# Ternary weights turned in pairs, rows turned by transfers, a split store and earlier norms

## The chip, the cores and the metric

One NeuronCore of a Trainium2 chip runs the whole program. The metric is the device time of one execution in microseconds; lower is better. TensorE, VectorE (DVE), ScalarE (ACT), GpSimd (POOL) and SyncE (SP, which issues most transfers) run side by side and are ordered by semaphores only.

## The reference

Four residual blocks on x of 1250 rows by 1024 (fp32), each on layer-normalised rows:

```python
x = x + layernorm(x) @ W.T + bias            # W scattered from 41250 edge weights at [src, dst]
x = x + moe(layernorm(x))                    # 8 experts, top 2, capacity 314, 1024 -> 512 -> 1024, relu
h = layernorm(x) @ gW.T + gb                 # dense linear layer
x = x + segment_sum(norm * h[col], row)      # normalised adjacency with self loops, norm from degrees
x = x + bitlinear(gelu(bitlinear(layernorm(x), w1)), w2)   # 1024 -> 4096 -> 1024

def _quant_weight(w):
    s = jnp.clip(jnp.mean(jnp.abs(w)), EPS, None)
    wq = jnp.clip(jnp.round(w / s), -1.0, 1.0) * s
    return w + jax.lax.stop_gradient(wq - w)
def _bitlinear(x, w):
    return jnp.einsum('bsi,oi->bso', _quant_act(x), _quant_weight(w))
```

So each feed-forward weight becomes -1, 0 or +1 times one scale: it is +1 above s/2 and -1 below -s/2. Activations are rounded to 8-bit integers by row.

## The kernel before

Rows are cut into NT = 10 tiles of 128; x stays in SBUF. The 1024 features make KD = 8 blocks of 128, the hidden 4096 make KF = 32. Every engine has its instruction stream written out by hand; the order in each stream and the semaphores set the order of the work. Values that need more than 16 bits are carried as two fp16 parts, high and low.

Stages in time: edges are turned into dense matrices (one-hot matmuls, L816 and L819, whose moving operand `o_key` has a step of SLOTS = 2 fp16 elements); first linear layer; router; eight experts; mixture of the experts' results; second linear layer; aggregation over the adjacency, with the ternary weights made beside it; feed-forward.

**Linear layers** (`normalised`, four functions of that name or its inlined form). Per tile n with buffer u = n % 2: POOL computes `rstd`; DVE `norm` writes `xn` (L1625); ACT `high` writes `xh` (L1230); DVE `low` writes `xl` (L1630). TensorE `transposes` turns `xh` and `xl` by eight 128x128 transposes each into PSUM banks 4 and 5 (L889, L895); ACT `copy_high` and DVE `copy_low` bring them to `xth` and `xtl` (L1234, L1634). `product` (L907) then runs 48 matmuls of 512 columns. TensorE does the transposes of tile i + 1 ahead of the product of tile i. DVE takes the result out (L1665 in the first layer, `h32` at L1933 in the second), and in the first layer statistics follow. In the first layer TensorE and ACT run tiles 0 to 7 and DVE tiles 0 to 5 as hardware loops over pairs of tiles (`pairs`, `peeled`); TensorE and ACT do so in the second layer too.

**Experts and mixture.** SP stores the three row groups of an expert's result (SM = 128, 128, 58 rows) to `eo_d`; the 58 rows are stored as two halves of columns (L567, L568). Once all stores have landed, POOL gathers two rows per token into `back` buffers (L761), four in flight; its stream is gather 0 to 3, `rstd` 0, gathers 4 and 5, `rstd` 1, gathers 6 and 7, `rstd` 2, and so on. DVE's `mixed(i, k)` adds each with its gate (L1889) and `mixed_statistics(i)` follows. DVE does tiles 0, 1, 2, then the norms of tiles 0 and 1, and the other mixtures one by one inside the linear layer's tiles, in this order: norm i+2, `hs_l` of tile i-1 (L1905), first half of mixture i+3, low i+2, second half, statistics, then `h32` of tile i, which waits for product i.

**Ternary pieces and aggregation.** The weights of both feed-forward layers come as 64 pieces of 128 rows by 1024 (fp32, 512 KB) into four buffers `fnat` (L585, L590); a load waits until the piece four before has been used. For piece n DVE makes `fneg` = (w < -s/2) one piece ahead (L1950) and `fq` = (w > s/2) - fneg in fp16 (L1960); `fq` has two buffers. TensorE turns it by eight transposes (L1056); ACT copies the result as fp8 into `w1q` or `w2q` (L1371). TensorE's stream aggregates ten tiles: four matmuls with the identity (L1066), then ten groups of six (L1070); in tiles 0 to 7 a piece's transposes follow groups 2 to 9. After the third piece of a tile DVE adds the previous tile's aggregate to x (`agg`, L1939) and takes statistics.

**Feed-forward.** TensorE multiplies `xqt` with `w1q` (L1084), ACT applies gelu (L1382), DVE quantises, transfers turn the rows (L604, L617), TensorE multiplies with `w2q` (L1113), 64 matmuls for each half of a tile.

Of the kernel before, what the change touches and what calls it, by code (L numbers as in the profile page):

```python
# [85 lines left out]
def build_kernel(nc, x_in, src_in, dst_in, ew_in, bias0_in, wg_in, w1_in, b1_in, w2_in, b2_in,  # L86
                 gw_in, gb_in, f1_in, f2_in, out):
    ctx = ExitStack()
    with ctx:
# [77 lines left out]
        xth = sb("ln", "xth", [P, 2, KD, P], F16)  # L167
        xtl = sb("ln", "xtl", [P, 2, KD, P], F16)
# [95 lines left out]
        w1q = sb("wide", "w1q", [P, KD, FH], F8)  # L264
        w2q = sb("wide", "w2q", [P, KF, D], F8)
# [6 lines left out]
        fq = sb("misc", "fq", [P, 2, D], F16)  # L272
        fneg = sb("misc", "fneg", [P, 2, D], F8)
# [22 lines left out]
        eo_d = nc.dram_tensor("eo_d", [NE * CAP, D], F32).ap()  # L296
        xq_d = nc.dram_tensor("xq_d", [2, KD * P, P], F16).ap()
# [50 lines left out]
        s_xth, s_xtl = sem("s_xth"), sem("s_xtl")  # L348
        s_mm = sem("s_mm")
# [38 lines left out]
        s_swm = sem("s_swm")  # L388
        s_fn = [sem(f"s_fn{i}") for i in range(4)]
        s_fneg = sem("s_fneg")  # L390
# [24 lines left out]

        def parts(n, u):
# [9 lines left out]
        def hold(eng):  # L426

            eng.sem_inc(s_held, 1)

# [26 lines left out]
        def _(sp):  # L456
# [89 lines left out]
            def expert(e, ep):  # L546
# [8 lines left out]
                for s in range(3):  # L555
# [19 lines left out]


# [62 lines left out]
            for u in range(2):  # L639
                sp.wait_ge(s_eout[u], 16 + 16 * 3 * NE // 2)  # L640
                sp.wait_ge(s_eoh[u], 16 + 16 * NE // 2)
# [4 lines left out]
        def _(pool):  # L646
# [106 lines left out]
            for u in range(2):  # L753
                pool.wait_ge(s_eout[u], 16 + 16 * 3 * NE // 2)
                pool.wait_ge(s_eoh[u], 16 + 16 * NE // 2)
# [16 lines left out]
        def _(pe):  # L772
# [108 lines left out]
            def transposes(n, u):  # L881
# [4 lines left out]
                if not isinstance(n, int) or n > 0:  # L886
                    pe.wait_ge(s_xth, n)
# [4 lines left out]
                if not isinstance(n, int) or n > 0:  # L892
                    pe.wait_ge(s_xtl, n)
# [3 lines left out]

            def product(n, u, rh, rl):


                pe.wait_ge(s_xth, n + 1)
                pe.wait_ge(s_xtl, n + 1)
# [8 lines left out]
            def normalised(r, body, peeled=2):  # L911

                transposes(r, 0)

                def step(i, u):
                    if not last_of(i, NT):
                        transposes(r + i + 1, 1 - u)
                    body(i, u)

                pairs(pe, step, peeled=peeled)  # L920
# [1135 lines left out]
```

## Time and profile before

| | us |
|---|---|
| median of 3 runs | 1209.96 |
| lowest, highest | 1209.90, 1210.97 |
| profiled execution | 1212.86 |
| its span, first to last instruction | 1211.1 |

| engine | busy us | share of the span |
|---|---|---|
| TensorE matmul | 1041.0 | 86% |
| VectorE | 787.6 | 65% |
| ScalarE | 439.5 | 36% |
| GpSimd | 162.2 | 13% |

Busy time is that of instructions of an engine; the chain that ended last is followed back from the last instruction, at each step to what released it. Durations of matmuls include their way through the array, so rates are read from starts. All times are from one profiled execution and count from the start of its span.

### The profile page before, as it was taken

To read this page: it belongs to the slowest core of one execution; us is meant where nothing else is said; L and a number is where in the kernel's file an instruction comes from. 1 tells how busy PE (TensorE), PEld (TensorE's weight loads), DVE (VectorE), ACT (ScalarE), POOL (GpSimd) and SP (SyncE) were. 2 spreads that over 40 slices of the span, in tenths; PEclk is the share of its full clock that TensorE was granted. 3 is DMA by queue.
4 is the path that set the end of the run, shared out by engine and by line. 5 is a ranking of instruction groups with operands and counts; after the bars stand their busy time and mean duration, and the time that the engine had idled before them with its cause. 6 is when DMAs were issued, how large, how long until landed. Compare 5 with 4: busy or idle time off the path is not lost.

```text
span 1211.1 us, 19022 instructions
## 1 busy us (share of the span) xinstructions
PE 1041.0 (86%) x7309; PEld 574.3 (47%) x7309; DVE 787.6 (65%) x1082; ACT 439.5 (36%) x510; POOL 162.2 (13%) x215
## 2 busy tenths in 40 slices
PE   0777599975699999987099989888889999999997
PEld 0666444434566666654055435444444444444443
DVE  7989667749655555564477728888883855555541
ACT  3389435426244444454031213433321322222111
POOL 5200233420311111100422000112110000000000
PEclk9999799997599999999599999999999999999999
DMA  4467334526467777743432116665621254554430
GB/s 155 160 215 264 82 136 156 193 80 252 150 204 259 263 252 263 263 171 102 143 102 73 35 40 221 208 196 183 203 77 22 49 126 110 124 119 116 104 87 31
DMA packets 138686, 181.35 MB, mean 150 GB/s; under 512 B 99209, under 2 KB 99531, under 8 KB 134527
## 3 DMA queue, kind: packets, MB, share of 16 engines
q1 hardware_dynamic: 129023, 158.12, 40.7%
q0 software_dynamic: 9600, 22.36, 6.0%
q8 instruction: 42, 0.69, 0.2%
q14 instruction: 21, 0.17, 0.0%
HBM read 137.78 MB, written 31.66 MB: 140 GB/s over the span
## 4 chain that ended last, share of the span: by engine, by line
PE 65%; DVE 17%; issue 7%; DMA 6%; ACT 3%; POOL 1%; DVEq 1%; ACTq 0%; SPq 0%; POOLq 0%
PE ps L907 12%; PE ps L1113 11%; PE ps L1084 11%; PE ps L1000 8%; PE ps L1018 7%; PE ps L1070 5%; DVE fq L1960 3%; DMA fnat_a<-in_L_ffn_w 3%; DVE stats L1484 2%; DVE xn L1625 2%; PE ps L974 1%; DVE w1l L1780 1%; PE ps L1056 1%; PE ps L855 1%; DMA back_a<-eo_d,slot_i 1%
## 5 line engine op out<-in xcount | busy, mean ns | idle before, releaser
L1113 PE MATMUL ps<-w2q,hqt 128*128 128x512 fp8e4 x640 | 140.8, 379 | 1.4 <-DVE out_t L2014 1.4
L1084 PE MATMUL ps<-w1q,xqt 128*128 128x512 fp8e4 x640 | 139.9, 379 | 1.4 <-issue 1.4
L1382 ACT ACTIVATE hf<-ps,fs 128x512 f32<-128x512 f32 x80 | 54.9, 687 | 183.2 <-PE ps L1084 183.2
L1995 DVE TENSOR_REDUCE hm<-hf 128x1 f32<-128x512 f32 x80 | 54.2, 685 | 76.3 <-ACT hf L1382 76.3
L1084 PEld LDWEIGHTS ps<-w1q,xqt 128*128 128x128 f16 x640 | 62.5, 98 | 76.7 <-issue 1.9
L1113 PEld LDWEIGHTS ps<-w2q,hqt 128*128 128x128 f16 x640 | 62.3, 98 | 75.8 <-DVE out_t L2014 1.9
L1000 PE MATMUL ps<-xdh,w1h 128*128 128x314 f16 x256 | 78.0, 304 | 3.5 <-DVE w1l L1780 2.7
L1000 PE MATMUL ps<-xdh,w1l 128*128 128x314 f16 x256 | 77.3, 302 | 0.0
L1000 PE MATMUL ps<-xdl,w1h 128*128 128x314 f16 x256 | 77.2, 302 | 0.0
L687 POOL TENSOR_TENSOR rtmp<-mv,consts 128x1 f32<-128x1 f32 x40 | 12.7, 318 | 455.3 <-DVE mv L1489 455.3
L1960 DVE SCALAR_TENSOR_TENSOR fq<-fnat_a,sw,fneg 128x1024 f16<-128x1024 f32 x48 | 61.5, 1281 | 7.2 <-PE ps L1056 7.2
L1070 PE MATMUL ps<-hs_h,at_h 128*128 128x512 f16 x200 | 60.4, 384 | 0.0
L1070 PE MATMUL ps<-hs_l,at_h 128*128 128x512 f16 x200 | 60.0, 382 | 0.0
L1070 PE MATMUL ps<-hs_h,at_l 128*128 128x512 f16 x200 | 59.9, 382 | 0.0
L1056 PE MATMUL ps<-id,fq 128*128 128x128 f16 x512 | 39.4, 220 | 23.7 <-DVE fq L1960 22.5
L816 PE MATMUL ps<-o_key,o_src 128*128 128x108 f16 (+1 forms) x432 | 37.1, 217 | 21.4 <-DVE o_key L1564 18.6
L1484 DVE BATCH_NORM_STATS2 stats<-x 128x6 f32<-128x512 f32 (+1 forms) x80 | 51.5, 685 | 5.3 <-DVE x L1889 0.9
L1056 PEld LDWEIGHTS ps<-id,fq 128*128 128x128 f16 x512 | 31.1, 98 | 47.8 <-DVE fq L1960 40.9
L1371 ACT ACTIVATE w1q<-ps 128x1024 fp8e4<-128x1024 f16 x32 | 32.7, 1023 | 55.2 <-PE ps L1056 55.2
L745 POOL DMA_INDIRECT gx<-xs_d,tok_i x24 | 26.9, 1120 | 191.1 <-PE ps L974 153.0
L1371 ACT ACTIVATE w2q<-ps 128x1024 fp8e4<-128x1024 f16 x32 | 32.7, 1023 | 53.4 <-PE ps L1056 53.4
L1230 ACT ACTIVATE xh<-xn 128x1024 f16<-128x1024 f32 x20 | 20.8, 1051 | 83.2 <-DVE xn L1625 83.2
(277 smaller groups left out, 2247.8 us busy)
## 6 DMA issues: line engine op xcount, KB each, us to landing
abs_in<-in_L_ffn_w SPq DMA_DIRECT2D x32, 1024.0 KB, 4.8
wstage<-in_L_ffn_w SPq DMA_DIRECT2D x32, 1024.0 KB, 10.2
fnat_a<-in_L_ffn_w SPq DMA_DIRECT2D x48, 512.0 KB, 4.4
eo_d<-eo SPq DMA_DIRECT2D x16, 512.0 KB
bias_b<-in_L_ffn_w SPq DMA_DIRECT2D x16, 512.0 KB, 3.6
hq_d<-hq SPq DMA_DIRECT2D x8, 1024.0 KB, 6.3
xs_d<-xs_all SPq DMA_DIRECT2D x10, 512.0 KB, 5.2
out_x<-out_t SPq DMA_DIRECT2D x9, 512.0 KB, 2.6
```

Source lines behind the costliest of these rows:

```text
L907: last = mm(ps[:, 2 * u + h, :], lhs[:, u, k, :], rhs[:, k, h * 512:(h + 1) * 512], start=(k == 0 and a == 0), stop=(k == KD - 1 and a == 2))
L1000: last = mm(ps[:, 6 + hb % 2, 0:CAP], lhs[:, k, hb * P:(hb + 1) * P], rhs[:, k, :], start=(k == 0 and a == 0), stop=(k == KD - 1 and a == 2))
L1018: last = mm(ps[0:m, (2 * s + h) % 3, :], lhs[:, k, s * P:s * P + m], rhs[:, k, h * 512:(h + 1) * 512], start=(k == 0 and a == 0), stop=(k ...
L1056: last = tr(bank16(4 + n % 4)[:, k * P:(k + 1) * P], fq[:, n % 2, k * P:(k + 1) * P], id16[:, :])
L1070: last = mm(ps[:, 2 * u + h, :], lhs[:, b, i * P:(i + 1) * P], rhs[:, b, h * 512:(h + 1) * 512], start=False, stop=(b == NT - 1 and a == 2))
L1084: last = mm(ps[:, n % 4, :], xqt[:, u, k, :], w1q[:, k, n * 512:(n + 1) * 512], start=(k == 0), stop=(k == KD - 1))
L1113: last = mm(ps[:, 4 + h, :], hqt[:, u, k, :], w2q[:, k, h * 512:(h + 1) * 512], start=(k == 0), stop=(k == KF - 1))
L1371: cp(part, bank16(4 + n % 4).rearrange("p (k c) -> p k c", k=KD), ACT.Copy, saturate=False).then_inc(s_fc, 1)
L1382: cp(hf[:, i % 2, n * 512:(n + 1) * 512], ps[:, n % 4, :], ACT.Gelu, scale=fs[:, i % 2, 3:4]).then_inc(s_ge, 1)
L1484: v.bn_stats(stats[:, h, :], x[:, i, h * 512:(h + 1) * 512]).then_inc(s_bn, 1)
L1960: v.scalar_tensor_tensor(out=fq[:, n % 2, :], in0=fnat[n % 4], scalar=sw[:, 4 + m:5 + m], in1=fneg[:, n % 2, :], op0=ALU.is_gt, op1=ALU.su ...
L1995: last = v.tensor_reduce(hm[:, u, n:n + 1], hf[:, u, n * 512:(n + 1) * 512], AX.X, ALU.max, apply_absolute_value=True)
```

## The change

Ternary pieces: `fq` is fp8, and two neighbouring values are turned as one 16-bit word, so a piece takes four transposes; ACT copies 512 16-bit words for 1024 values. `w1q` and `w2q` keep each pair side by side, so a matmul reads them with a step of two bytes, and `xq` is written in the matching order. For three pieces in four ACT computes sign(w + s/2) into `fsgn` (four buffers) and DVE takes min((w > s/2), sign); for the fourth DVE still compares itself, no longer a piece ahead.

Second linear layer: tiles 0 and 1 are turned as before. From tile 2 on SP stores `xh` and `xl` to `xt_d` in runs of 128 elements, waits for both, and reads them back with one turning transfer into `xt`, once the product that used the buffer is done.

The expert's 58-row stores are split into 48 and 10 rows: four stores. The third mixture comes after the norms, lows and first copy of tiles 0 and 1. The loops over tiles in the first and second linear layers are written out.

```diff
-        xth = sb("ln", "xth", [P, 2, KD, P], F16)
-        xtl = sb("ln", "xtl", [P, 2, KD, P], F16)
+        xt = sb("ln", "xt", [P, 2, 2, KD, P], F16)
+        xth, xtl = xt[:, :, 0, :, :], xt[:, :, 1, :, :]
...
-        w1q = sb("wide", "w1q", [P, KD, FH], F8)
-        w2q = sb("wide", "w2q", [P, KF, D], F8)
+        w1q = sb("wide", "w1q", [P, KD // 2, FH, 2], F8)
+        w2q = sb("wide", "w2q", [P, KF // 2, D, 2], F8)
...
-                        sp.dma_start(expert_rows[e][s * P:CAP, 0:512], eo[0:SM[s], u, 0:512]).then_inc(s_eout[u], 16)
-                        sp.dma_start(expert_rows[e][s * P:CAP, 512:D], eo[64:64 + SM[s], u, 512:D]).then_inc(s_eoh[u], 16)
+                        rows, rest = expert_rows[e][s * P:s * P + 48, :], expert_rows[e][s * P + 48:CAP, :]
+                        sp.dma_start(rows[:, 0:512], eo[0:48, u, 0:512]).then_inc(s_eout[u], 16)
+                        sp.dma_start(rest[:, 0:512], eo[48:SM[s], u, 0:512]).then_inc(s_eoh[u], 16)
+                        sp.dma_start(rows[:, 512:D], eo[64:64 + 48, u, 512:D]).then_inc(s_eoh[u], 16)
+                        sp.dma_start(rest[:, 512:D], eo[64 + 48:64 + SM[s], u, 512:D]).then_inc(s_eoh[u], 16)
...
+            def rows_out(n):
+                u = n % 2
+                sp.wait_ge(s_xh, n + 1)
+                sp.wait_ge(s_xl, n + 1)
+                for a, part in enumerate(parts(n, u)):
+                    sp.dma_start(xt_d[u].rearrange("(a k p) c -> a p k c", a=2, p=P)[a],
+                                 part.rearrange("p (k c) -> p k c", c=P)).then_inc(s_xrow, 16)
+            def rows_turned(n):
+                u = n % 2
+                sp.wait_ge(s_mm, n)
+                sp.wait_ge(s_xrow, 32 * moved(n) + 32)
+                if moved(n) > 0:
+                    sp.wait_ge(s_xt, 16 * moved(n))
+                sp.dma_start(xt[:, u, :, :, :].rearrange("p a k c -> p (a k c)"), xt_d[u], transpose=True).then_inc(s_xt, 16)
+            for i in range(NT):
+                if by_transfer(R_LIN1 + i + 1) and i + 1 < NT:
+                    rows_turned(R_LIN1 + i + 1)
+                if i + 2 < NT:
+                    rows_out(R_LIN1 + i + 2)
...
-                for k in range(KD):
-                    last = tr(bank16(4 + n % 4)[:, k * P:(k + 1) * P], fq[:, n % 2, k * P:(k + 1) * P], id16[:, :])
+                packed = fq[:, n % 2, :].bitcast(F16)
+                for k in range(KD // 2):
+                    last = tr(bank16(4 + n % 4)[:, k * P:(k + 1) * P], packed[:, k * P:(k + 1) * P], id16[:, :])
...
-                        last = mm(ps[:, n % 4, :], xqt[:, u, k, :], w1q[:, k, n * 512:(n + 1) * 512],
+                        last = mm(ps[:, n % 4, :], xqt[:, u, k, :], w1q[:, k // 2, n * 512:(n + 1) * 512, k % 2],
...
+            def upper_sign(n):
+                act.wait_ge(s_fn[n % 4], 16 * (n // 4) + 16)
+                if n >= 4:
+                    act.wait_ge(s_fq, 4 + n - 3)
+                cp(fsgn[:, n % 4, :], fnat[n % 4], ACT.Sign, bias=sw[:, 4 + n // 32:5 + n // 32],
+                   saturate=False).then_inc(s_fsgn, 1)
...
             for n in range(64):
+                if n + 2 < 64 and signed(n + 2):
+                    upper_sign(n + 2)
                 act.wait_ge(s_ft, 2 + n + 1)
...
-            for i in range(3):
+            for i in range(2):
                 mixed(i, 0)
                 mixed(i, 1)
                 mixed_statistics(i)
...
             copy_low(R_LIN1, 0)
+            mixed(2, 0)
+            mixed(2, 1)
+            mixed_statistics(2)
...
             def weight_piece(n):
-                m = n // 32
-                if n < 63:
-                    below(n + 1)
-                dve.wait_ge(s_fneg, n + 1)
+                m, k = n // 32, n // 4
+                if signed(n):
+                    dve.wait_ge(s_fsgn, n - k + 1)
+                else:
+                    dve.wait_ge(s_fn[n % 4], 16 * k + 16)
+                    v.tensor_scalar(fsgn[:, n % 4, :], fnat[n % 4], sw[:, 6 + m:7 + m], 1.0, ALU.is_lt, ALU.mult,
+                                    saturate=False).then_inc(s_fneg, 1)
+                    dve.wait_ge(s_fneg, k + 1)
                 dve.wait_ge(s_ft, n + 1)
                 v.scalar_tensor_tensor(out=fq[:, n % 2, :], in0=fnat[n % 4], scalar=sw[:, 4 + m:5 + m],
-                                       in1=fneg[:, n % 2, :], op0=ALU.is_gt, op1=ALU.subtract).then_inc(s_fq, 1)
+                                       in1=fsgn[:, n % 4, :], op0=ALU.is_gt, op1=ALU.min if signed(n) else ALU.subtract,
+                                       saturate=False).then_inc(s_fq, 1)
```

`signed(n)` is `n % 4 != 3`, `by_transfer(n)` is `n >= R_LIN1 + 2`, and `moved(n)` counts the tiles turned by transfer before tile n.

## Rows read from the trace of the kernel before

**Rows 1.** page: shares of the chain that ended last, by engine

```profile
PE 65%; DVE 17%; issue 7%; DMA 6%; ACT 3%; POOL 1%; DVEq 1%; ACTq 0%; SPq 0%; POOLq 0%
```

**Rows 2.** chain in order of time (start us, us, what), feed-forward stage

```profile
1023.27 13.81 PE ps L1084 x64
```

**Rows 3.** the same chain, first linear layer

```profile
168.65 2.70 DVE xn L1625
...
226.53 2.82 DVE xn L1625
```

**Rows 4.** timeline (start us, us, engine, line): last small store, first gather

```profile
571.71 0.31 SPq L568 DMA_DIRECT2D eo_d<-eo  x1
...
579.55 0.94 POOL L761 DMA_INDIRECT back_a<-eo_d,slot_i  x1 [85.64 <-DMA eo_d<-eo]
```

**Rows 5.** DMA issues: queue, count, KB each, median us from issue to landing

```profile
fnat_a<-in_L_ffn_w SPq DMA_DIRECT2D x48, 512.0 KB, 4.4
...
out_x<-out_t SPq DMA_DIRECT2D x9, 512.0 KB, 2.6
...
xq_d<-xq SPq DMA_DIRECT2D x10, 256.0 KB, 3.5
...
xqt<-xq_d SPq DMA_TRANSPOSE x10, 3.1
...
hqt<-hq_d SPq DMA_TRANSPOSE x8, 6.3
```

**Rows 6.** timeline, statistics and norms ahead of the second linear layer

```profile
593.78 0.17 DVE L1489 COPY mv<-mv_one 128x2 f32<-128x2 f32 x1
...
595.37 0.19 POOL L691 TENSOR_TENSOR rstd<-rtmp,consts 128x1 f32<-128x1 f32 x1
...
602.24 1.53 DVE L1625 TENSOR_SCALAR xn<-x,mv,rstd 128x1024 f32<-128x1024 f32 x2
```

**Rows 7.** chain in order of time, second linear layer

```profile
608.76 10.89 PE ps L907 x48
...
620.54 10.36 PE ps L907 x48
...
699.31 20.73 PE ps L907 x96
```

**Rows 8.** one stretch: us, busy by engine, clock, DMA share, GB/s

```profile
643.00:654.30 11.30, 11.30 (x66) 5.60 (x64) 9.07 (x12) 3.01 (x3) 2.90 (x5) 1.00 0.29 93
```

**Rows 9.** chain in order of time, aggregation

```profile
723.98 1.87 PE ps L1066 x4
...
745.38 3.88 PE ps L1070 x18
...
875.27 3.88 PE ps L1070 x18
```

**Rows 10.** timeline, two ternary pieces on TensorE

```profile
732.80 0.65 PEld L1056 LDWEIGHTS ps<-id,fq 128*128 128x128 f16 x8
...
734.54 0.54 PEld L1056 LDWEIGHTS ps<-id,fq 128*128 128x128 f16 x6
```

**Rows 11.** groups by line: out<-in, count, busy us, mean ns, idle before

```profile
L1960 DVE SCALAR_TENSOR_TENSOR fq<-fnat_a,sw,fneg 128x1024 f16<-128x1024 f32 x48 | 61.5, 1281 | 7.2 <-PE ps L1056 7.2
...
L1950 DVE TENSOR_SCALAR fneg<-fnat_a,sw 128x1024 fp8e4<-128x1024 f32 x48 | 36.1, 753 | 11.2 <-DMA fnat_a<-in_L_ffn_w 10.0
...
L1371 ACT ACTIVATE w1q<-ps 128x1024 fp8e4<-128x1024 f16 x32 | 32.7, 1023 | 55.2 <-PE ps L1056 55.2
...
L1166 ACT ACTIVATE st_c<-ps 128x480 f16<-128x480 f32 x27 | 15.4, 571 | 14.0 <-issue 7.0 <-PE ps L819 5.9 <-PE ps L816 1.1
...
L1356 ACT ACTIVATE hs_h<-h,dinv 128x1024 f32 x8 | 9.2, 1149 | 67.6 <-DVE h L1933 67.6
```

**Rows 12.** timeline, first stage: first and last of eleven such matmuls

```profile
50.11 0.21 PE L816 MATMUL ps<-o_key,o_src 128*128 128x108 f16 x1
...
50.86 0.21 PE L816 MATMUL ps<-o_key,o_src 128*128 128x108 f16 x1
```

More of the change, by code:

```diff
@@ L414, in build_kernel, with turned, moved, by_transfer @@
         R_GNN0, R_MOE, R_LIN1 = 0, NT, 2 * NT
+        FIRST = 2
+        def turned(n):
+            return n
+        def moved(n):
+            return n - R_LIN1 - FIRST
+        def by_transfer(n):
+            return n >= R_LIN1 + FIRST
         def parts(n, u):
@@ L885, in transposes @@
                 pe.wait_ge(s_xh, n + 1)
-                if not isinstance(n, int) or n > 0:
-                    pe.wait_ge(s_xth, n)
+                if n > 0:
+                    pe.wait_ge(s_xth, turned(n))
                 for k in range(KD):
@@ L891, in transposes @@
                 pe.wait_ge(s_xl, n + 1)
-                if not isinstance(n, int) or n > 0:
-                    pe.wait_ge(s_xtl, n)
+                if n > 0:
+                    pe.wait_ge(s_xtl, turned(n))
                 for k in range(KD):
@@ L909, in product, with normalised @@
                 last.then_inc(s_mm, 1)
-            def normalised(r, body, peeled=2):
+            def normalised(r, body):
                 transposes(r, 0)
[L915 to L920, printed above, removed]
+                for i in range(NT):
+                    if i + 1 < NT and not by_transfer(r + i + 1):
+                        transposes(r + i + 1, 1 - i % 2)
+                    body(i, i % 2)
             pe.wait_ge(s_built, 1)
@@ L1112, in ffn_out @@
                         for h in range(2):
-                            last = mm(ps[:, 4 + h, :], hqt[:, u, k, :], w2q[:, k, h * 512:(h + 1) * 512],
+                            last = mm(ps[:, 4 + h, :], hqt[:, u, k, :], w2q[:, k // 2, h * 512:(h + 1) * 512, k % 2],
                                       start=(k == 0), stop=(k == KF - 1))
@@ L1240, in normalised @@
                 copy_high(r, 0)
-                def step(i, u):
-                    if not last_of(i, NT):
+                for i in range(NT):
+                    u = i % 2
+                    if i + 1 < NT and not by_transfer(r + i + 1):
                         act.wait_ge(s_mm, r + i + 1)
                         copy_high(r + i + 1, 1 - u)
-                    if not last_of(i, NT, 2):
-                        act.wait_ge(s_tl, r + i + 1)
+                    if i + 2 < NT:
+                        rows_read(r + i)
                         high(r + i + 2, u)
                     body(i, u)
-                pairs(act, step)
             act.wait_ge(s_built, 1)
             def gnn0(i, u):
-                if not last_of(i, NT, 2):
+                if i < KD:
                     for k in range(2):
@@ L1632, in copy_low, with normalised @@
             def copy_low(n, u):
-                dve.wait_ge(s_tl, n + 1)
+                dve.wait_ge(s_tl, turned(n) + 1)
                 v.tensor_copy(xtl[:, u, :, :].rearrange("p k c -> p (k c)"), bank16(5)).then_inc(s_xtl, 1)
-            def normalised(r, body, peeled=2):
+            def normalised(r, body):
                 norm(r, 0, 0)
@@ L1642, in normalised @@
                 copy_low(r, 0)
-                def step(i, u):
-                    if not last_of(i, NT):
+                for i in range(NT):
+                    u = i % 2
+                    if i + 1 < NT and not by_transfer(r + i + 1):
                         dve.wait_ge(s_mm, r + i + 1)
                         copy_low(r + i + 1, 1 - u)
-                    if not last_of(i, NT, 2):
+                    if i + 2 < NT:
                         norm(r, i + 2, u)
@@ L1653, in step @@
                     body(i, u)
-                pairs(dve, step, peeled=peeled)
             def pair_banks(u):
@@ L1912, in _ @@
             copy_low(R_LIN1, 0)
+            mixed(2, 0)
+            mixed(2, 1)
+            mixed_statistics(2)
             for i in range(NT):
                 u = i % 2
-                if i + 1 < NT:
+                if i + 1 < NT and not by_transfer(R_LIN1 + i + 1):
                     dve.wait_ge(s_mm, R_LIN1 + i + 1)
```

69 lines of the change are left out of this document (44 added, 25 removed).

## The prediction

> **What bounds the kernel now.** I read the chain that ended last first: 65% of the span is TensorE, 17% VectorE, 6% DMA [rows 1]. So TensorE is the engine to relieve, and the places where the chain leaves it are the stages to look at. The feed-forward stage is pure TensorE: 64 matmuls of 512 columns take 13.81 us, with no break [rows 2]; it has 20 such blocks, 276 us. Four places before it matter. In the first linear layer the chain runs through VectorE's `xn` once a tile: five tiles from 168.65 to 226.53, 11.58 us each [rows 3]. Between experts and second linear layer TensorE idles: the last small store is issued at 571.71, the first gather leaves at 579.55 [rows 4], the norms of tile 0 start at 602.24 [rows 6], the first product at 608.76 [rows 7]. In that linear layer TensorE is the bound: a product takes 10.36 us, but from tile 1 (620.54) to tile 8 (699.31) it is 11.25 us a tile [rows 7], the rest being 16 transposes of the next tile; VectorE is busy 9.07 of 11.30 us beside it [rows 8]. In the aggregation with the ternary pieces a tile takes (875.27 - 745.38) / 6 = 21.65 us [rows 9]. TensorE's own work there is 13.82 us of matmuls and 8 pieces: two pieces start 1.74 us apart with six matmuls (1.295 us) between [rows 10], so a piece's eight transposes cost 0.44 us, 17.4 us in all. The other 4.3 us TensorE waits.
>
> **The change, part by part.**
>
> *First linear layer, loops written out.* In the loop each tile takes 11.58 us; what the same work costs with TensorE as the bound is 11.25 [rows 3, 7]. Written out, the instructions lose their register operations, which lie on VectorE's chain. Six tiles at 0.32: **1.9 us**, between 0 (the chain stays) and 2.
>
> *Last store in four.* The two stores of 58 rows, 116 KB each, let the gather go 7.8 us after the second was issued [rows 4]; stores of 128 rows with four times the bytes land in 2.6, and 256 KB in short runs in 3.5 [rows 5]. It is the 58 rows that cost, not the bytes. With 48 and 10 rows there are four issues of 0.31 us, two more than before, so the last goes out at 572.3 and lands at about 574.8: the gathers start at 575.05, **4.5 us** earlier. If the 10-row stores stayed as slow in proportion to rows, 1.3 us would be lost of it; ends 2.5 and 5.3. In the seven experts before, no wait of TensorE hangs on a store; nothing there.
> The Trainium skill (DMA: Bandwidth & Descriptors, "Why a DMA increments its semaphore by 16 and not by 1") says that the largest number up to 16 which divides the slowest dimension is the number of engines used: 2 for 58 rows, 16 for 48, 10 for 10. The trace agrees as far as 7.8 against 2.6 us go. By it the gain is the same 4.5 us.
>
> *Norms ahead of the third mixture.* Statistics of tile 1 end at 593.95, its `rstd` at 595.56, yet the norms begin at 602.24 [rows 6], since the third mixture stands in front, waiting for its gathers. Now norm 0 starts at 593.95, norm 1 when POOL has `rstd`, 595.65 to 596.45; then low 0 and low 1 (1.2 us each), with TensorE's transposes and the copies behind them as now. From norm to product it was 6.52 us [rows 6, 7]; with the wait for `rstd` I count 6.65. The product starts at 600.6: **8.1 us**. What moves behind is mixture 2 (two operations and statistics, 4.4 us); VectorE then has norm 2 at 605.5 and low 2 at 608.5 with product 0 ending at 611.5, and gathers 8 and 9 leave 3 us later than relative to the norms before; their mixture comes 4 us after they land. Ends: 5 and 8.5.
>
> *Rows turned by transfers.* TensorE drops the transposes of eight tiles: 8 x (11.25 - 10.36) = **7.1 us**, and ScalarE and VectorE one PSUM copy each a tile. In place: SP issues two stores of 256 KB (short runs) and one turning transfer of 512 KB. The nearest rows are 3.5 us for such a store, 3.1 and 6.3 us for a turn of 256 KB and 1 MB [rows 5], hence about 4.2 for 512 KB. Let T be the end of product i-1. `xl` of tile i+2 is ready at T + 6.3 (`h32` 1.2, then ScalarE's 1.15 for `hs_h` with norm i+2 beside it, `hs_l` 1.3, half a mixture and low 1.2 each, gaps); the two stores land by T + 11; the turn waits for product i (T + 10.4) too and lands by T + 15.5; product i+2 needs it at T + 20.7. Five us spare, with the DMA engines 29% busy now [rows 8]. Queued behind these waits on SP is only the next tile's pair; the weight loads come after the last product anyway. VectorE falls to 8.5 of 10.4 us, so it doesn't become the bound. Ends: 2 (each tile late by 0.6) and 7.2.
> The Trainium skill speaks against this part: DMA: Bandwidth & Descriptors, "Specifications", gives 512 B as the least run for full rate, with read-modify-write below, and these runs are 256 B. By it the stores would be slow; the trace has 256 KB in such runs in 3.5 us [rows 5], which is slow for its bytes and yet early enough.
>
> *Ternary pieces.* Per piece TensorE has four transposes for eight: 0.22 us for 0.44, so 15.6 us a tile. VectorE keeps the 1.28 us operation (1.31 with its gap) and does the 0.75 us comparison only for one piece in four [rows 11]; there it is no longer a piece ahead, so it counts 0.82. ScalarE takes the sign for three in four. Its nearest row is the 1.149 us of a 1024-wide activation with a pointer operand [rows 11] (without one 1.02). Its copy halves: 480 elements out of PSUM took 0.571 us [rows 11], so 0.6; reading every second 2-byte word it could be up to 1.02. ScalarE: 6 x 1.15 + 8 x 0.6 = 11.7 us a tile (15.1 at the upper end). VectorE: 8 x 1.31 + 2 x 0.82 + 3.2 for aggregation and statistics = 15.3. No engine is full; the order decides. VectorE may be only two pieces ahead of the transposes, so piece 2 starts about 5 us into the tile and is followed by the 3.2 us of aggregation and then piece 3 with its comparison, done at 11.8 where TensorE wants it at 9.3: 2.5 us idle. Piece 7, the other with a comparison, costs 0.8. That makes 15.6 + 3.3 = 18.9. A buffer's round is load 4.4 [rows 5] (0.8 more is my allowance for loads close together), issue 0.35, sign 1.15, ternary 1.3: 7.2 to 8.0 us for four pieces, 2.0 each at most, under the mean 2.4, but it bites where pieces come close together: I take 19.1. Seven tiles at 21.65 - 19.1 = 2.5 give 17.5; the first tile, without an aggregation in it, 745.38 - 0.86 - 723.98 = 20.5 before [rows 9], gains about 1.5: **19 us**. Ends: 13 (copy 1.02, transposes at 0.3, loads slower) and 22.
>
> *Feed-forward.* `w1q` and `w2q` are read with a step of two bytes. Nothing in that stage had one. The nearest is the key matrix of the first stage, read with a step of four bytes: ten pairs of 108 + 48 columns take 0.75 us [rows 12], 75 ns each, against 66 ns at the rate of [rows 7]; the 9 ns are spread over two matmuls and two weight loads. I take 0 and not the 14%, which for 276 us would be 38. `xq` read in another order costs VectorE at most 0.5 us a tile in a stage in which it waits.
>
> **The sum.** 1.9 + 4.5 + 8.1 + 7.1 + 19 = 40.6 us. The profiled execution took 1212.9 us (span 1211.1); 1172.3 follows for it. The median of the runs shown is 2.9 lower: **1169.4 us**.
>
> **Rivals.**
> 1. *Loads become the bound of the aggregation.* The sign stands between landing and ternary operation, on an engine that also waits for transposes in order. For it: the chain already passes through `fnat_a` loads, 4.4 us each [rows 5]. Against: the round above. If loads land in 6.5 us when close together, a tile takes 20.4: 10 us gained there, total 1178.
> 2. *Turned rows late.* Store, wait, turn in series beside 1 MB of gathers a tile. From `xl` on there are 14.4 us (I count 9.2); each one beyond costs 8 over the tiles. At 15.3 the 7.1 are gone, 1176; at 17.4, 24 are lost, 1193.
> 3. *Slower than before: strided moving operand.* Price 2.76 us for each per cent on 276 us [rows 2]. From 15% on it eats all 40.6 us and the kernel is slower; at half rate it takes 1445. The rows at twice the step [rows 12] allow at most 14%, all of the excess put down to it.
> 4. *A part doesn't do what it says:* the sign and the copy alternate at the cost of a function-table load, or ScalarE's chain of sign and copy exceeds TensorE's pace. For the latter 15.1 us a tile is the upper end and the gain 13: 1175.
>
> **How the numbers follow.** Forecast (all parts within their ends, 1163 to 1176): 0.68. Loads bound: 0.12. Turned rows late: 0.08. Table loads or another part lost: 0.06, mostly still faster. Strided operand: 0.06. For 8 in 10 the range takes in the forecast, the loads and the milder late turns: **1161 to 1182**. About 0.2% (2.4 us) is what can be told from no change: faster 0.93, same 0.01, slower 0.06.
>
> **What would show it.** Right: first gather some 4.5 us sooner after the last store; `xn` 0 directly after the second statistics; products of tiles 2 to 9 back to back at 10.36 us; aggregation period near 19 us with TensorE waiting once or twice a tile for `fq`, after the aggregation; the feed-forward blocks still 13.81. Wrong: TensorE waiting for `xt` transfers, ScalarE's sign waiting for loads at nearly every piece, blocks over 13.9 us in the feed-forward stage.

## The result and the profile after

The changed kernel takes 1177.86 us (median of 4 runs, 1174.06 to 1180.31) against 1209.93 for the kernel before, a ratio of 0.972 (95% interval 0.970 to 0.974): 32 us faster. Forecast were 1169.4 us and a range of 1161 to 1182. The profiled execution took 1174.06 us where the sum said 1172.3 (its span, first to last instruction, is 1172.3 by chance). Cut into the same six stretches, the two profiled executions compare so (us):

| stretch | before | after | gain | forecast |
|---|---|---|---|---|
| start to the last expert's second layer | 567.1 | 564.8 | 2.3 | 1.9 |
| from there to the first gather | 12.4 | 7.8 | 4.6 | 4.5 |
| first gather to first product of the second linear layer | 29.0 | 21.05 | 8.0 | 8.1 |
| first product to first matmul of the aggregation | 115.4 | 111.9 | 3.5 | 7.1 |
| aggregation with ternary pieces | 200.65 | 180.3 | 20.4 | 19 |
| feed-forward to the end | 286.5 | 286.4 | 0 | 0 |
| sum | 1211.1 | 1172.3 | 38.8 | 40.6 |

The 2.3 us of the first row are not what 1.9 stood for: the first expert starts only 0.4 us earlier (324.99 for 325.41). The rest lies in the last expert, where TensorE waits for a weight load in both kernels (3.1 and 2.5 us). Behind that wait the same 24 matmuls ran at a granted clock of 0.69 before and of 1.00 after (start us, us, what):

```profile
545.34 4.72 PE ps L1000 x24
...
544.51 3.23 PE ps L1052 x24
```

In a second execution of the changed kernel they took 4.89 us at 0.65, so this is scatter and the agreement of the row is luck.

First the page's chain shares, that is the shares of the chain of work that ended last, which answer to [rows 1]; then, of the chain in order of time (start us, us, what), the first linear layer [rows 3], the second [rows 7], two tiles of the aggregation [rows 9] and a feed-forward block [rows 2]:

```profile
PE 72%; DVE 14%; issue 5%; DMA 4%; ACT 2%; POOL 1%; SPq 1%; DVEq 0%; ACTq 0%; POOLq 0%
...
171.76 10.36 PE ps L963 x48
...
228.51 10.36 PE ps L963 x48
...
617.68 11.24 DMA xt<-xt_d
628.97 72.71 PE ps L963 x336
...
744.20 3.88 PE ps L1123 x18
...
762.25 3.88 PE ps L1123 x18
...
781.98 3.88 PE ps L1123 x18
...
1012.13 13.81 PE ps L1137 x64
```

VectorE is off the chain of the first linear layer: its tiles follow at 11.35 us, not 11.58. In the second a transfer of turned rows stands on the chain for 11.24 us, and the seven products behind it run without a break, 72.71 us for 336 matmuls, 10.39 a tile. The feed-forward blocks are 13.81 us as before.

Timeline rows (start us, us, engine, line) for [rows 4] and [rows 6, 7]: the last of the four stores, the first gather, norm 0, norm 1, first product.

```profile
570.23 0.35 SPq L594 DMA_DIRECT2D eo_d<-eo  x1
...
572.62 0.95 POOL L811 DMA_INDIRECT back_a<-eo_d,slot_i  x1 [78.74 <-DMA eo_d<-eo]
...
586.80 0.81 DVE L1700 TENSOR_SCALAR xn<-x,mv,rstd 128x1024 f32<-128x1024 f32 x1
...
588.91 0.85 DVE L1700 TENSOR_SCALAR xn<-x,mv,rstd 128x1024 f32<-128x1024 f32 x1 [1.30 <-POOL rstd L741]
...
593.67 1.06 PE L963 MATMUL ps<-gwt_h,xt 128*128 128x512 f16 x2
```

From the last store to the first gather it is 2.39 us, where it was 7.84. Norm 0 follows the second statistics with nothing in between, as forecast, and norm 1 waited 1.30 us for POOL's `rstd`. Groups by line, for [rows 11] (count, busy us, mean ns, idle before):

```profile
L2032 DVE SCALAR_TENSOR_TENSOR fq<-fnat_a,sw,fsgn 128x1024 fp8e4<-128x1024 f32 x48 | 60.7, 1283 | 33.4 <-ACT fsgn L1426 17.9 <-PE ps L1109 15.5
L1426 ACT ACTIVATE fsgn<-fnat_a,sw 128x1024 fp8e4<-128x1024 f32 x48 | 54.9, 1143 | 21.0 <-DMA fnat_a<-in_L_ffn_w 20.8
...
L1445 ACT ACTIVATE w2q<-ps 128x512 int16<-128x512 int16 x32 | 18.9, 591 | 23.1 <-PE ps L1109 23.1
L1441 ACT ACTIVATE w1q<-ps 128x512 int16<-128x512 int16 x32 | 18.9, 590 | 21.8 <-PE ps L1109 21.8
```

The sign takes 1.143 us (forecast 1.15), the int16 copy of half as many elements 0.59 (forecast 0.6), the ternary operation 1.283 as ever. One load of a function table stands between 600 and 900 us, ahead of the gelu; none belongs to the sign.

### The profile page after: what moved, and what is told of

Same layout as the page of the kernel before. It is cut to its first block, busy times and chain, and to the rows that moved or that the text cites. A ratio compares the mean times of both kernels' runs of the same rounds, so it can differ in the third digit from the quotient of the medians.

```text
span 1172.3 us, 18075 instructions
## 1 busy us (share of the span) xinstructions
PE 1016.9 (87%) x6925; PEld 555.2 (47%) x6925; DVE 749.9 (64%) x1026; ACT 454.2 (39%) x550; POOL 158.3 (14%) x215
## 4 chain that ended last, share of the span: by engine, by line
PE 72%; DVE 14%; issue 5%; DMA 4%; ACT 2%; POOL 1%; SPq 1%; DVEq 0%; ACTq 0%; POOLq 0%
PE ps L963 15%; PE ps L1166 12%; PE ps L1137 12%; PE ps L1123 9%; PE ps L1052 8%; PE ps L1070 7%; DVE fq L2032 2%; PE ps L1026 1%; DVE stats L1559 1%; DVE w1l L1853 1%; PE ps L905 1%; PE ps L1109 1%; DMA xt<-xt_d 1%; DMA gx<-xs_d,tok_i 1%; PE ps L885 1%
## 5 line engine op out<-in xcount | busy, mean ns | idle before, releaser
L963 PE MATMUL ps<-gwt_h,xt 128*128 128x512 f16 x320 | 83.5, 382 | 2.7 <-DMA xt<-xt_d 2.7
L963 PE MATMUL ps<-wt_h,xt 128*128 128x512 f16 x320 | 83.9, 380 | 0.0
L2032 DVE SCALAR_TENSOR_TENSOR fq<-fnat_a,sw,fsgn 128x1024 fp8e4<-128x1024 f32 x48 | 60.7, 1283 | 33.4 <-ACT fsgn L1426 17.9
L1426 ACT ACTIVATE fsgn<-fnat_a,sw 128x1024 fp8e4<-128x1024 f32 x48 | 54.9, 1143 | 21.0 <-DMA fnat_a<-in_L_ffn_w 20.8
L1559 DVE BATCH_NORM_STATS2 stats<-x 128x6 f32<-128x512 f32 x80 | 51.5, 685 | 5.0 <-DVE at_l L1650 0.4
L963 PEld LDWEIGHTS ps<-gwt_h,xt 128*128 128x128 f16 x320 | 31.5, 99 | 41.1 <-DMA xt<-xt_d 3.5
```

The costliest lines, as they stand in the source:

```text
L963: last = mm(ps[:, 2 * u + h, :], lhs[:, u, k, :], rhs[:, k, h * 512:(h + 1) * 512], start=(k == 0 and a == 0), stop=(k == KD - 1 and a == 2))
L1426: cp(fsgn[:, n % 4, :], fnat[n % 4], ACT.Sign, bias=sw[:, 4 + n // 32:5 + n // 32], saturate=False).then_inc(s_fsgn, 1)
L1559: v.bn_stats(stats[:, h, :], x[:, i, h * 512:(h + 1) * 512]).then_inc(s_bn, 1)
L2032: v.scalar_tensor_tensor(out=fq[:, n % 2, :], in0=fnat[n % 4], scalar=sw[:, 4 + m:5 + m], in1=fsgn[:, n % 4, :], op0=ALU.is_gt, op1=ALU.mi ...
```

## Experiments

All ratios are to the kernel before, run beside them on the same chip; medians of 4 runs (5 where said, 10 for the loops written out). Three chips were used, on which the kernel before had medians of 1209.7, 1211.1 and 1211.1 us, so a difference of two rows in us can be off by 1.4 us from that alone. Stretches are those of one profiled execution of each kernel.

| kernel | us | ratio, 95% interval |
|---|---|---|
| changed kernel again | 1177.28 | 0.972 (0.968 to 0.977) |
| before, loops written out | 1209.01 | 1.000 (0.998 to 1.001) |
| no transfers | 1179.13 | 0.974 (0.971 to 0.977) |
| transfers from tile 5 | 1174.62 | 0.970 (0.967 to 0.972) |
| two parts undone (store, norms) | 1184.38 | 0.978 (0.975 to 0.981) |
| pairs without the sign | 1190.18 | 0.982 (0.978 to 0.986) |
| all pieces by the sign | 1168.41 | 0.963 (0.958 to 0.968) |
| half of each weight load left out | 1176.35 | 0.970 (0.966 to 0.975) |
| sums read earlier | 1159.74 | 0.959 (0.954 to 0.965) |
| the same, half loads | 1152.14 | 0.952 (0.949 to 0.955) |
| the same, transfers from tile 5 (5 runs) | 1162.89 | 0.959 (0.957 to 0.962) |
| that, all pieces by the sign (5 runs) | 1162.08 | 0.959 (0.957 to 0.962) |

### What the written-out loops give

The kernel before with the peeling of its first linear layer set to all ten tiles on every engine (VectorE's line; those of TensorE and ScalarE likewise):

```diff
-            normalised(R_GNN0, gnn0, peeled=4)
+            normalised(R_GNN0, gnn0, peeled=NT)
```

> The kernel before with only the tile loops of the first linear layer (TensorE, ScalarE, VectorE) and ScalarE's in the second written out. Forecast: 1.9 us faster than before (1208), tiles 1 to 7 at 11.28 to 11.35 us in place of 11.58. The changed kernel's trace shows 3.8 us at the end of that layer, of which 1.4 were there before its first product and 0.8 in that product: if these belong to the edit, 3.8 us faster up to there; if they are chance, 1.5 to 2. Rival: what is gained there is given back in the gathers ahead of the experts, as the changed kernel's trace has it (3.4 us given back), and the time is within 0.5 us of before.

The layer's last products start at 240.04 us where they started at 243.65, yet the first expert's matmuls begin at 324.37 instead of 325.41, and the medians differ by 0.7 us (1209.01, and 1209.74 on the same chip), no more than the measurement can tell. Of these 3.6 us 2.3 were there before the layer's first product (147.91 for 150.18), ahead of the loops that were written out; in the changed kernel and its variants, with one code up to there, that product starts anywhere from 147.6 to 150.1. The layer itself, from its first product to its last ones, gained 1.3 us here and 1.7 and 2.4 us in two executions of the changed kernel, so 1.9 was right for the stage. Behind it 2.6 us are given back: the three gathers of `gx` are issued at 307.72, 310.98 and 313.07 against 310.62, 311.97 and 314.05, the first of them taking POOL 2.96 us for 1.05. What reaches the median is not told from nothing; by the interval it is between 2.3 us won and 1.1 lost.

### Turned rows: worth 7 us, or 2, or a loss

The changed kernel again, for the spread between executions, and without transfers (all tiles turned on TensorE):

```diff
-        FIRST = 2
+        FIRST = 10
...
-                if i + 2 < NT:
+                if i + 2 < NT and by_transfer(R_LIN1 + i + 2):
                     rows_out(R_LIN1 + i + 2)
```

> The changed kernel once more, unedited. Its four runs lay in two pairs, 1174 to 1176 and 1180 us, and the profiled execution is of the fast pair. Theory: what differs between executions is when turning transfers and weight loads land, so another execution has another number of waits for xt in the second linear layer (one of 3.2 us in the first profile) and other long tiles in the aggregation (18.05 and 19.7 us in turn there); median 1174 to 1180. Rival: the difference lies elsewhere (first stage, router, experts); then the second linear layer lasts 111.9 us from its first product to the first aggregation matmul and the aggregation 178.8 us again, within 1 us.

> The changed kernel with all ten tiles of the second linear layer turned on TensorE, as before; everything else stays. Theory: turning by transfer gave 3.3 us of the forecast 7.1, since the transfers share the DMA engines with the gathers (share 0.8 to 1.2 there, 0.29 before) and one product waits. Then this kernel is 3 to 4 us slower than the changed one in the execution compared, the layer lasts 115 us and the DMA share falls back to 0.3. Rival, the transfers give the full 7 us and the loss has another cause: 7 us slower. Rival, the contention costs more than it gives in most executions: this kernel is as fast or faster.

Without transfers the layer takes 116.5 us, and the median is only 1.9 us above, less than the two intervals can tell apart. Waits of TensorE in the changed kernel's second execution, and the stretch cut at that wait (us, busy by engine, clock, DMA share, GB/s):

```profile
PE ps L963 <- DMA xt<-xt_d: 4.3, 1, 4.3
...
610.00:616.40 6.40, 6.40 (x31) 2.74 (x28) 5.67 (x8) 0.11 (x1) 1.52 (x3) 1.00 1.13 163
616.50:620.80 4.30, 0.04 (x1) 0.00 (x0) 3.65 (x4) 2.09 (x2) 2.93 (x4) 0.87 1.18 188
620.90:627.00 6.10, 6.10 (x16) 2.25 (x17) 4.68 (x7) 0.00 (x0) 0.85 (x3) 0.54 0.77 235
```

TensorE stands 4.3 us, and afterwards the granted clock is 0.54, mostly the lower level of 1.2 GHz, for 6 us: 16 matmuls where 31 ran in the 6.4 us before. The layer took 115.1 us here, 3.2 more than in the other execution. There, the wait was 2.7 us and the clock stayed at 1.00. What the DMA engines did, in the first execution (window cut at the late transfer):

```profile
600.00:610.00 10.00, 10.00 (x48) 4.58 (x47) 8.70 (x11) 2.62 (x3) 4.34 (x6) 1.00 0.80 208
610.00:620.00 10.00, 10.00 (x48) 4.48 (x47) 8.06 (x11) 2.09 (x2) 3.16 (x5) 1.00 0.96 213
...
617.70:628.90 11.20, 8.57 (x40) 3.68 (x38) 8.76 (x12) 2.93 (x4) 4.00 (x6) 1.00 1.14 184
...
DMA to landing us min/median/max: 4.3/5.9/11.2
```

A share of 0.80 to 1.14, where 0.29 stood in [rows 8]. That 0.29 was the gathers alone; without transfers the share is 0.20 to 0.50 in this layer, and with transfers behind the last gather (660 to 680 us) it is 0.52 to 0.55. The stores and turns thus bring a share of about 0.5 of their own, which the forecast did not count. The turn issued at 617.68 (tile 3) beside gathers at 616.26 and 617.59 landed after 11.2 us; the least was 4.3, the most in any kernel 14.3.

The rows of tile 3 also went out late. `xl` was ready at 611.7, but SP was held by the issue of the turn before, and the first store left at 613.66 (start us, us, what):

```profile
608.34 5.22 SPq L619 DMA_TRANSPOSE xt<-xt_d  x1
```

The seven profiled executions of kernels with both the norms ahead and transfers from tile 2 all had such waits, 1.5 to 5.8 us in sum, for tile 2, 3 or 4, and took 111.2 to 117.9 us for this layer, mean 114.1. That gathers make the turns slow is argued from their times; no run leaves them out. Two ways to take the collision away were run.

Transfers only for tiles 5 to 9, by the same edit with FIRST = 5:

> The changed kernel, with tiles 0 to 4 of the second linear layer turned on TensorE as before and only tiles 5 to 9 by transfers. Theory (the gathers crowd the transfers): in two traces of the changed kernel the gathers of the mixture run until about 660 us, the DMA engines are 80 to 119% busy by the row of 600 to 660, and one turned tile came late, by 2.7 us in one execution and by 4.3 us in the other, where the granted clock then fell to 0.5 and cost some 4 us more. Tile 5's rows are turned after most gathers are through, so no product waits and five tiles save 0.9 us each, 4.5 us: a median near 1174.6 us (kernel without transfers 1179.1, minus 4.5), and the stretch from the first product to the aggregation takes 116.3 - 4.5 = 111.8 us with no wait for xt. Rival (each transfer costs TensorE something, or the transposing transfer is slow whatever runs beside it): some product waits again, and the median stays at 1177 to 1179 us.

As the theory said, 1174.6 us; 111.98 us for the layer, and TensorE never waits for `xt`. The gain of 2.7 us over eight tiles at risk lies within the intervals, and the kernels under "Both mended" don't repeat it.

The last store in two, and the third mixture ahead of the norms again, with the transfers from tile 2 as they are (the stores as in L567 and L568 of the kernel before):

```diff
-            for i in range(2):
+            for i in range(3):
                 mixed(i, 0)
...
             copy_low(R_LIN1, 0)
-            mixed(2, 0)
-            mixed(2, 1)
-            mixed_statistics(2)
```

> The changed kernel without two of its parts: the last expert's rows are stored in two transfers as before, and the third tile's mixture stands ahead of the norms again. Theory (the two terms are what the stretches of the two traces say): from the start of the last expert's products of 2.73 us to the first gather's issue 12.4 us again in place of 7.8, from that issue to the first product some 29 us in place of 21, together 12.7 us: a median near 1190 us. Rival (what the two parts gave is partly taken back by the gathers falling further into the linear layer's first tiles, where turned tiles then come late): without them the wait for a turned tile and the lower clock behind it are gone too, and the median is near 1184 us.

The rival's number came, 1184.4, 7.1 us above the changed kernel's second runs and not 12.7. The stretches are back at 7.84 us from store to gather (570.77 to 578.61) and 28.4 to the first product (607.03), so both terms were right. But now the linear layer takes 108.1 us, with no wait for `xt`. Chain row, three windows, and landings:

```profile
607.24 103.98 PE ps L960 x480
...
607.00:617.00 10.00, 10.00 (x48) 4.51 (x46) 6.68 (x9) 1.56 (x2) 2.39 (x5) 0.96 0.54 156
617.00:627.00 10.00, 10.00 (x48) 4.55 (x47) 8.12 (x9) 2.10 (x2) 0.94 (x1) 1.00 0.92 199
627.00:637.00 10.00, 10.00 (x48) 4.51 (x46) 8.20 (x10) 2.09 (x2) 3.16 (x5) 1.00 0.75 203
...
DMA to landing us min/median/max: 4.4/6.3/7.2
```

480 matmuls without a break, though the share is 0.92 in one window: a high share alone doesn't make a turn late, and here none took over 7.2 us. Tile 2's rows are stored 4.2 us after the first product's start (611.25), against 8.5 in the changed kernel (602.19 after 593.67), where the third mixture now stands in between and the gathers are earlier in the layer too. Against 115.4 us before, the transfers gain 7.3 us, the 7.1 of the sum. The parts are not additive: with store and norms changed, which bring 12.6 us, the transfers keep about half of their gain or less (3.5 and 0.3 us in the changed kernel's two executions). That it is the norms and not the split store was only argued from the order of the rows; the two weren't undone singly.

### The ternary pieces

Pairs alone: every piece's comparison by VectorE, one piece ahead, as before (`below` makes `fsgn` of piece n + 1).

```diff
-            return n % 4 != 3
+            return False
...
-            for n in range(2):
-                upper_sign(n)
...
+                    if n < 63:
+                        below(n + 1)
+                    dve.wait_ge(s_fneg, n + 1)
```

> The changed kernel with ternary pieces still turned in pairs, but both comparisons on VectorE, one piece ahead as before; ScalarE computes no sign. Theory: VectorE's 2.0 us a piece was the pace, so pairs alone give little: aggregation period 20.5 to 21.5 us, the kernel 14 to 19 us slower than the changed one (1190 to 1196). Rival, the halved transposes and copies carry the gain: period under 20 us, less than 8 us slower.

The aggregation takes 191.9 us: the pairs give 8.8 of its 20.4 us, the sign the other 11.6. The first figure is uncertain by some 3 us, since the same stage took 200.7 us in the profiled execution of the kernel before and 197.4 in that of the written-out loops, which leave it as it is.

What bounds the 18.9 us that a tile takes now? Its tiles alternate, 18.05 and 19.73 us. Two neighbouring tiles of the changed kernel (us, busy by engine, clock, DMA share, GB/s), the one wait in the second, and all of TensorE's waits from 744 to 858 us:

```profile
744.20:762.20 18.00, 15.72 (x97) 7.98 (x96) 12.94 (x15) 9.54 (x14) 2.77 (x3) 1.00 0.67 207
762.20:782.00 19.80, 17.52 (x98) 8.50 (x96) 15.53 (x16) 12.33 (x16) 2.76 (x3) 0.91 0.76 246
...
772.97 0.40 PE L1109 MATMUL ps<-id,fq 128*128 128x128 f16 x4 [2.28 <-DVE fq L2032]
...
774.23 1.06 PE L1123 MATMUL ps<-hs_h,at_l 128*128 128x512 f16 x2
...
PE ps L1109 <- DVE fq L2032: 13.8, 6, 2.4
```

One wait of 2.3 us a tile, at the piece behind the reading of the previous tile's sums, as forecast. After every second one the granted clock falls (pairs of matmuls at 1.06 us for 0.59) and costs 1.7 us more; the sum didn't have this.

Half of each load left out, from the fifth piece on:

```diff
-                    sp.dma_start(fnat[u], f1v[j, u]).then_inc(s_fn[u], 16)
+                    sp.dma_start(fnat[u][:, 0:512], f1v[j, u][:, 0:512]).then_inc(s_fn[u], 16)
```

> The changed kernel, with each piece of the feed-forward weights from the fifth on loaded in its first half of columns only, so the other half stays what the buffer held: a quarter MB each instead of half, the rest of the work is the same. Theory B (the loads bound the aggregation): a load lands in 5.0 us now, in some 3.5 then; with four buffers in the ring that takes 1.5 us off every fourth piece, 3 us off a tile, 24 us of the aggregation, the median near 1155 us. Theory A (VectorE's order bounds it, the load only sets the alternation between 18.05 and 19.73 us): the tile goes to 18.05 throughout, 6 to 7 us in all, the median near 1171 us.

Nothing changes. TensorE's waits are the same to the tenth, 13.8 us in six, while ScalarE's for loads are all but gone (1.0 us); the alternation stays, so it is no matter of loads either:

```profile
PE ps L1112 <- DVE fq L2035: 13.8, 6, 2.4
...
ACT w2q L1448 <- PE ps L1112: 33.6, 20, 3.3
```

The sums of the previous tile read one piece earlier, in the 3.9 us at a tile's start in which TensorE takes no piece and VectorE, two pieces ahead, waits for it:

```diff
-                    if k == 2 and i > 0:
+                    if k == 1 and i > 0:
                         agg(i - 1, (i - 1) % 2)
```

> The changed kernel, with VectorE reading the previous tile's sums (3.9 us: one addition, two statistics) after the second ternary piece of a tile instead of after the third. Theory A (the order on VectorE bounds what is left of the aggregation): at a tile's start TensorE works 3.9 us without taking a piece, while VectorE, two pieces ahead, idles; then it takes the third piece and spends 3.9 us on the sums while TensorE runs out of pieces (waits of 16.1 us in seven tiles of the trace). Put into the idle time, the reading costs nothing: 2 us of each of seven tiles, 14 us of 178.8, limited by VectorE's own 16.7 us of work a tile against 18.9: a median near 1164 us. Theory B (the loads of the pieces bound): the tile stays at 18 to 19.7 us and the median at 1176 to 1178 us.

17.5 us less than the changed kernel, by one digit. The aggregation itself is 167.4 us for 180.3 and 178.4, so 11 to 13 us shorter, near the 14 expected; the other 5 to 7 us of the median lie outside the stage the edit touches. The clock no longer falls. The expectation misread VectorE's work: its 16.7 us a tile counted each of the two statistics at the 1.30 us that the chain gives both together (14.3 busy in the windows). Four tiles average 17.5 us. TensorE's waits, a window, and ScalarE's waits:

```profile
PE ps L1109 <- DVE fq L2032: 9.0, 17, 1.0
...
762.84:780.10 17.26, 16.30 (x98) 7.72 (x97) 14.21 (x16) 10.81 (x15) 2.79 (x4) 1.00 0.75 244
...
ACT fsgn L1426 <- DMA fnat_a<-in_L_ffn_w: 22.9, 16, 3.4
```

No wait of TensorE is over 1.0 us now, in all 9.0 for 13.8, the clock is 1.00, and ScalarE waits 22.9 us for loads. Is that the next bound?

> The kernel with the earlier reading, and each piece of the feed-forward weights from the fifth on loaded in its first half of columns only, so the other half stays what the buffer held. Halving the loads alone changed nothing, since the order on VectorE made TensorE wait 16.1 us in seven tiles with either size. Theory (with that order mended the loads are the next bound, as ScalarE's waits for them, 22.9 us, suggest): the tile of 17.5 us comes to TensorE's own 16.1, 10 us in all, a median near 1150 us. Rival (what is left is the order of sign, comparison and copy on VectorE and ScalarE): under 0.5 us a tile, a median of 1156 to 1159 us.

Yes. With half loads the aggregation falls from 167.4 to 156.4 us and TensorE waits for nothing, which is the theory's 10 us and one more (7.6 us in the medians). Seven tiles in a row take 15.60 us, TensorE's own work as the forecast had it:

```profile
744.00:858.00 114.00, 114.00 (x673) 57.45 (x671) 95.09 (x111) 60.02 (x81) 15.15 (x24) 1.00 0.37 109
```

The same cut that gave nothing in one order gives 11 us of this stage in the other.

All comparisons by the sign:

```diff
-            return n % 4 != 3
+            return True
...
-                    dve.wait_ge(s_fsgn, n - k + 1)
+                    dve.wait_ge(s_fsgn, n + 1)
```

> The changed kernel, with the lower comparison of every piece by ScalarE's sign, the fourth ones too. VectorE's work falls from 16.7 to 14.1 us a tile, ScalarE's rises from 11.7 to 13.9. Theory A (VectorE's total work bounds the tile of 18.9 us on average): 2.6 us less in each of eight tiles, the median near 1160 us. Theory B (the order of the work, or the loads, bound it): the comparison was done in time in which VectorE would wait anyway; one wait more on ScalarE for each load, the median within 3 us of 1177.

9 us less than the changed kernel: between the two theories. The aggregation takes 169.8 us, 8.6 to 10.5 less; taking the comparison out of the piece behind the sums shortens the same wait (10 waits, 12.0 us, none over 1.7, for 7 of 16.1 between 724 and 870), and the clock stays at 1.00, which can make up the rest. On top of the earlier reading it gives little:

> As the kernel with both edits, and every piece's lower comparison by ScalarE's sign. With the earlier reading a tile takes 17.5 us on average, in which VectorE is busy 14.3 and TensorE 16.1. Theory (the two comparisons left on VectorE, 0.75 us each, still sit between the pieces and make TensorE wait): without them the tile comes to TensorE's own 16.1 us, 1.4 us less in each of seven tiles, 10 us: a median near 1147 us. Rival (the loads are next: in the kernel with the earlier reading ScalarE's sign waits 22.9 us for them in 134 us, and VectorE 15.3 us for ScalarE): with one sign more in four behind the loads the gain is under 3 us, 1154 to 1158 us, or it is a loss of as much.

1162.1 against 1162.9 without it: the rival, though the median lies above its range. The aggregation took 165.8 us for 169.3 in the two profiled executions, but no gain shows in the medians. ScalarE waits 21.4 us for loads and VectorE 32.9 us for ScalarE (from 708 to 870 us).

### Both mended

The earlier reading (k == 1) and FIRST = 5 together:

> The two edits that helped, together: VectorE reads the previous tile's sums after the second piece of a tile, and only tiles 5 to 9 of the second linear layer are turned by transfers. Theory (they act in different stretches and add up): 1159.7 us less the 2.7 us that the later transfers gave alone (1174.6 against 1177.3) = 1157 us. Rival (the median of 1159.7 comes from executions in which the early transfers did not stall, and nothing is left to gain): 1159 to 1160 us.

Not 1157 but 1162.9, the same ratio, 0.959, as with the earlier reading alone. The layer takes 110.5 us with no wait for `xt`, but the profiled execution with the earlier reading alone had only 1.5 us of waits and took 111.2. Its runs went from 1158.4 to 1170.4 us, those of this kernel from 1160.1 to 1164.0. So the later transfers left the median as it was; whether they narrow the spread can't be said, since it rests on one run of four at 1170.4. Why the gain seen at 1174.6 is not seen again stays open; it may not have been one. Part is that the work ahead of this layer varies by itself: the first product starts between 592.9 and 596.0 us in eleven profiled executions with the same code up to there, and the aggregation took 169.3 us here for 167.4. Either version beats the changed kernel by 1.2 to 1.5% and the kernel before by 4.1%.

## Why the prediction was right, and where not

**First linear layer.** The tiles came at 11.35 us, not 11.25, and the stage gained 1.3 to 2.4 us, as said. What was wrong is that this reaches the end: the gathers that follow took most of it back, and the first expert starts 1.0 and 0.4 us earlier in two executions and 0.1 us later in a third. The 2.3 us of the table's first row have another source, the last expert.

**Last store.** 4.5 said, 4.6 found. The split stores land in 1.6 us, the gather leaves 2.4 after the last. By the Trainium skill's rule on the count of engines (DMA: Bandwidth & Descriptors, "Why a DMA increments its semaphore by 16 and not by 1") 58 rows use 2 engines, 48 rows 16 and 10 rows 10. The trace agrees with it as far as times go: 7.84 to 2.39 us with the rows cut 48 and 10. No loss from the 10-row stores, the lower end of 2.5, was seen.

**Norms ahead.** 8.1 said, 8.0 found, and 7.4 in the kernel with the parts undone (28.4 against 21.05).

**Turned rows: the step that failed.** The term, 7.1 us, was right for the transfers alone (7.3). What failed is "five us spare". It took a turn at 4.2 us, read from transfers with no gathers beside them, and the DMA engines at the 29% of the gathers alone; with the stores and turns themselves the share is 0.8 to 1.2, and a turn took 4.3 to 14.3 us. It took the issue of a turn on SP at nothing, while it held SP for up to 6.3 us, and the next tile's stores waited behind it (1.9 us for tile 3). And the start was one of a settled tile (`xl` at T + 6.3), while tile 2, with the mixture moved behind the norms, has its rows at 8.5. For tile 3 of the changed kernel the 7.0 us of the longer turn and the 1.9 us on SP outweigh the 5.2 us spare, and TensorE waits 2.7. Rival 2 had the mechanism, with a chance of 0.08, but as a delay of every tile; it was one wait or two, with the lower clock behind it in some executions: 3.5 us kept in one, 0.3 in the other. That store and norms use up the slack of the transfers was in no term.

**Ternary pieces.** 19 said, 20.4 found, by the mechanism named: one wait after the sums (2.5 said, 2.3 found), sign and copy at their prices, VectorE 14.2 us a tile for 15.3. Loads were no bound in this order of the work (rival 1): halving them gave nothing. The 0.8 us at piece 7 did not show; the fall of the clock in every second tile, 0.9 us a tile, stands in its place, so the 18.9 us found against the 19.1 said are partly luck. So is the total: against the 197.4 us that this stage took in the kernel with its loops written out, the gain is 17 us.

**Feed-forward.** 0 said and found; rival 3 is out, and with it the main way to a slower kernel.

**The median.** 1177.9 for 1169.4 while the profiled executions agree to 1.8 us: the sum took off 2.9 us because the profiled execution of before lay so far above its median; that of after lies 3.8 below. The turned rows are part of it: the execution profiled was a mild one, and the second, at 1177.2 us, has 3.2 us more there and 1.9 us more ahead of this layer. The scatter of the aggregation in the kernel before, 3.3 us, is another part; the rest is not traced.

## To carry to other kernels

Two edits that each hold their price alone can share one slack: when one edit moves work earlier, recount the slack of every transfer that runs beside the next stage, at the DMA share it will have then, the new transfers' own included, and with the time that each issue holds its queue. Of a stage in which several engines alternate, look for the engine that idles just ahead of where it is then late: moving one reading by one piece took 11 to 13 us off the aggregation, and before that move halved loads gave nothing. A wait of TensorE can cost more than its length, by what the clock takes afterwards. And where a stretch agrees with its forecast, look inside it: here one agreed by luck.

## Of the hardware, not expected

- A turning transfer of 512 KB landed in 4.3 us at the least and, early in the layer beside gathers, in up to 14.3, with the DMA engines' share between 0.8 and 1.2 in the changed kernel. Its issue held SP for 1.5 to 6.3 us.
- A wait of 2.3 us lowered TensorE's clock in every second tile of the aggregation (granted 0.91 over the tile, 1.7 us lost), one of 2.7 us in the linear layer did not, and one of 4.3 did, for some 6 us. In the last expert the clock was 1.00 behind a wait of 2.5 us and 0.65 behind one of 2.6. Waits up to 1.0 us, seventeen of them, and ten of up to 1.7, left it at 1.00.
- A moving operand read with a step of two bytes in fp8 cost nothing: 13.81 us for 64 matmuls of 512 columns with and without.
- The first gather of `gx` held POOL for 2.96 us in all thirteen profiled executions of kernels with their loops written out, for 1.05 in the one of the kernel before, and so gave back most of what had been won ahead of it. Why is open.
